# First layer's query and key weights multiplied into one matrix on chip; V buffers zeroed by transfers

## The reference, cut to what matters

```python
h = film(rmsnorm(x, norm1_w), cond, film1_w, film1_b)      # x * (1 + scale) + shift, per batch entry
Q = h @ q_w + q_b
K = h @ k_w + k_b
V = h @ v_w + v_b
scores = jnp.einsum('bnd,bmd->bnm', Q, K) * D ** (-0.5)
attn = jax.nn.softmax(scores, axis=-1)
out = jnp.einsum('bnm,bmd->bnd', attn, V)
x = x_in + (out @ proj_w + proj_b)
```

## Time and profile before

| | us |
|---|---|
| median of 3 runs | 182.25 |
| lowest and highest | 182.13, 182.42 |
| the profiled execution | 182.43 |
| its span in the trace | 180.7 |

### The profile page before, as it was taken

One profiled execution on the slowest core, in us unless ns is written; L12 is line 12 of the kernel. 1 busy time (PEld: TensorE's weight loads), 2 busy tenths in 40 slices (PEclk: granted clock), 3 DMA queues, 4 the chain that ended last, 5 costly groups with the idle time before them and its releaser, 6 DMA issues.

```text
span 180.7 us, 5691 instructions
## 1 busy us (share of the span) xinstructions
PE 172.1 (95%) x2250; PEld 133.9 (74%) x2250; DVE 116.0 (64%) x349; ACT 107.7 (60%) x274; POOL 107.5 (59%) x176
## 2 busy tenths in 40 slices
PE   6988999999999999989999999999899999999994
PEld 6965888587485798767678876888788765668594
DVE  0694569978106069867756878768688556696333
ACT  2338858871993651667576766767877596623500
POOL 5499979899910905995005333359979877690000
PEclk9999999999999999999999999999999999999999
DMA  4999999702247200300110001100000000001103
GB/s 111 341 425 429 424 421 426 337 13 39 51 175 308 102 0 4 120 7 3 62 39 32 2 5 64 64 2 5 5 7 7 5 0 5 0 0 58 62 0 116
DMA packets 5334, 19.31 MB, mean 107 GB/s; under 512 B 572, under 2 KB 1292, under 8 KB 3980
## 3 DMA queue, kind: packets, MB, share of 16 engines
q1 hardware_dynamic: 4988, 18.27, 26.2%
q10 hardware_dynamic: 320, 0.68, 1.2%
HBM read 7.24 MB, written 1.09 MB: 46 GB/s over the span
## 4 chain that ended last, share of the span: by engine, by line
PE 47%; POOL 26%; issue 17%; DVE 6%; DMA 3%; ACT 0%; POOLq 0%; ACTq 0%
PE ps L328 8%; PE ps L337 7%; PE ps L315 6%; PE ps L307 6%; PE ps L265 4%; POOL gtmp L1222 4%; POOL xb L1224 4%; POOL xc L1217 3%; POOL xn L1252 3%; POOL rstd L1143 3%; PE ps L239 3%; POOL xs L1231 3%; DMA xs<-x 3%; POOL gated L1228 3%; PE ps L270 2%
## 5 line engine op out<-in xcount | busy, mean ns | idle before, releaser
L1028 DVE TENSOR_REDUCE nm<-ps 128x4 f32<-128x512 f32 x64 | 42.1, 683 | 17.1 <-PE ps L380 16.6
L765 ACT ACTIVATE shared<-ps 128x512 f32<-128x512 f32 x64 | 34.5, 596 | 18.8 <-PE ps L380 18.8
L380 PEld LDWEIGHTS ps<-k_pad,q_pad 32*128 32x128 f32 x512 | 29.7, 186 | 9.7 <-issue 5.9
L380 PE MATMUL ps<-k_pad,q_pad 32*128 32x128 f32 x512 | 35.0, 282 | 1.7 <-DVE nm L1028 1.3
L380 PE MATMUL ps<-q_pad,k_pad 32*128 32x128 f32 x512 | 35.0, 283 | 0.0
L380 PEld LDWEIGHTS ps<-q_pad,k_pad 32*128 32x128 f32 x512 | 29.3, 186 | 0.4 <-issue 0.2
L1143 POOL TENSOR_TENSOR rstd<-var_eps,half 128x4 f32<-128x4 f32 x16 | 16.4, 1025 | 20.9 <-DVE var_eps L886 15.2
L1228 POOL TENSOR_TENSOR gated<-attn,gate 128x128 f32<-128x128 f32 x16 | 7.3, 459 | 27.2 <-ACT attn L784 27.2
L446 PE MATMUL ps<-shared,vx 128*32 128x128 f32 x512 | 17.3, 275 | 0.3
L813 ACT ACTIVATE hid<-ps,W 128x512 f32<-128x512 f32 x16 | 10.9, 688 | 9.7 <-PE ps L328 9.7
L446 PEld LDWEIGHTS ps<-shared,vx 128*32 128x32 f32 x512 | 13.1, 109 | 3.0 <-issue 1.5
(11 more groups left out here) (135 smaller groups left out, 330.6 us busy)
## 6 DMA issues: line engine op xcount, KB each, us to landing
q_pad<-hid SPq DMA_DIRECT2D x1, 4096.0 KB, 21.9
k_pad<-hid SPq DMA_DIRECT2D x1, 4096.0 KB, 30.9
gate<-gates SPq DMA_DIRECT2D x1, 2048.0 KB, 6.6
xs<-x SPq DMA_DIRECT2D x4, 256.0 KB, 6.6
gate<-mask SPq DMA_DIRECT2D x1, 1024.0 KB, 11.8
q_pad<-apT SPq DMA_DIRECT2D x4, 256.0 KB, 2.4
k_pad<-apT SPq DMA_DIRECT2D x4, 256.0 KB, 2.4
W<-weights SPq DMA_DIRECT2D x1, 768.0 KB, 9.9
```

Source lines behind the costliest of these rows:

```text
L380: return mm(bank(to)[:, t], held[some, t, b], moved[some, t, b], start=True, stop=True, skip_group_check=True)
L765: a(pT[b % 2][:, r], bank(of), ACT.Exp, scale=HD ** -0.5).then_inc(s["c_exp"], 1)
L1028: v.tensor_reduce(nm[b % 2][:, 4 * r:4 * r + 4], bank(of), AX.X, ALU.max, negate=True).then_inc(s["c_max"], 1)
```

## The change

- **Weights.** The packed weights hold the transposes of Q's and K's weights. At the start PE multiplies them: `key_mat` is the product of the two matrices, `query_key` is K's weights times Q's bias, `key_row` is Q's weights times K's bias, and `query_bias` is the product of the two biases. The scores are then (h M + query_key) h plus a term for each row of the scores, and no K is computed: the scores' second operand is `hT` itself.
- **Key bias.** It adds a constant to each row of the scores. It comes out of V's product as its 129th column. The fourth entry of V lies in another bank (2), since four times 129 columns don't fit one.
- **Row maximum.** PSUM holds the scores without the row term; VectorE takes the maximum, then computes from it the true maximum (`amax`) and back from that the offset for the exponential (`emax`), two small instructions (`a_true`), after a wait for V's copy. ScalarE now evicts the query (it was VectorE) and V in two instructions, V of group 0 after the affine of group 1.
- **Start.** The folding products stand before the first transposes on PE, and ScalarE copies their result before its first affine. Group 1's normalisation is split between GpSimd and ScalarE. GpSimd makes both bias columns before its first root.
- **V buffers.** The two memsets of `vx` on GpSimd go. SyncE fills both buffers by two transfers of 1024 KB, issued behind the fills of the pads and ahead of the wait for all of them. The zeros lie in the upper half of `gate` instead of `hid[1]`, so ScalarE's wait for the fills goes. GpSimd waits for all four fills and writes the ones after its fourth layer-0 bias addition.

```diff
@@ SyncE
-            zeros = hid[1][:].rearrange("p f b n -> p (f b n)")
+            zeros = gate[:, B // 2:B].rearrange("n b g c -> n (b g c)")
             sp.wait_ge(s["zero_ok"], 1)
             for to in (q_pad, k_pad):
                 sp.dma_start(to[:].rearrange("p t b n -> p t (b n)"), zeros.unsqueeze(1).broadcast_to((128, 4, B * N)))\
                     .then_inc(s["pad_zero"], 16)
 
-            sp.wait_ge(s["pad_zero"], 32)
+            for to in vx:
+                sp.dma_start(to[:].rearrange("n b z -> n (b z)"), zeros).then_inc(s["pad_zero"], 16)
+
+            sp.wait_ge(s["pad_zero"], 64)
             sp.wait_ge(s["aug_ok"], 3)
@@ TensorE
-            def a_qk(g, n):
-
-                if n == 0:
-                    pe.wait_ge(s["a_h"], g + 1)
-                    pe.wait_ge(s["a_hd"], 1)
-                mm(ps[:, 1 + n, :], w("qk"[n]), hT[g % 2][:], start=True, stop=True).then_inc(s[("a_Q", "a_K")[n]], 1)
+            def a_query(g):
+
+                pe.wait_ge(s["a_h"], g + 1)
+                pe.wait_ge(s["a_hd"], 1)
+                pe.wait_ge(s["fold_ok"], 1)
+                if g:
+                    pe.wait_ge(s["a_qT"], g)
+                mm(ps[:, 1, :], key_mat, hT[g % 2][:], start=True, stop=True).then_inc(s["a_Q"], 1)
 
             def a_value(g):
                 pe.wait_ge(s["wvp_ok"], 1)
+                if g:
+                    pe.wait_ge(s["a_v"], g)
                 for j in range(G):
-                    ins = mm(bank(3)[:, j], hT[g % 2][:, j], wvp[:], start=True, stop=True, skip_group_check=True)
+                    to = ps[:, 3, 129 * j:129 * j + 129] if j < 3 else ps[:, 2, 0:129]
+                    ins = mm(to, hT[g % 2][:, j], wvp, start=True, stop=True, skip_group_check=True)
                 ins.then_inc(s["a_V"], 1)
 
             def a_scores(g):
                 u = g % 2
                 pe.wait_ge(s["a_qT"], g + 1)
-                pe.wait_ge(s["a_kT"], g + 1)
                 for j in range(G):
-                    ins = mm(bank(4 + 3 * u)[:, j], qT[u][:, j], kT[u][:, j], start=True, stop=True, skip_group_check=True)
+                    ins = mm(bank(4 + 3 * u)[:, j], qT[u][:, j], hT[u][:, j], start=True, stop=True, skip_group_check=True)
                 ins.then_inc(s["a_S"], 1)
                 pe.wait_ge(s["a_v"], g + 1)
...
             warm(6)
+            pe.wait_ge(s["w_attn0"], 16)
+            pe.wait_ge(s["qcol_ok"], 1)
+            at = 2 * N
+            for lhs, rhs, size in ((w("qt"), col("cols0", COL["k_b"]), 1), (w("qt"), w("kt"), C),
+                                   (w("kt"), col("cols0", COL["q_b"]), 1), (qcol[:], col("cols0", COL["k_b"]), 1)):
+                ins = mm(ps[:, 6, at:at + size], lhs, rhs, start=True, stop=True, skip_group_check=True)
+                at += size
+            ins.then_inc(s["fold_mm"], 1)
             a_first_norm()
...
-            a_qk(0, 0)
-            a_qk(0, 1)
+            a_query(0)
+            pe.wait_ge(s["a_xa"], 1)
+            a_norm(1)
             a_value(0)
-            a_norm(1)
             a_scores(0)
             for g in range(3):
-                a_qk(g + 1, 0)
-                a_qk(g + 1, 1)
+                a_query(g + 1)
                 a_value(g + 1)
@@ ScalarE
+            def a_q(g):
+                act.wait_ge(s["a_Q"], g + 1)
+                a(qT[g % 2], bank(1), ACT.Identity, bias=query_key).then_inc(s["a_qT"], 1)
+
+            def a_v(g):
                 act.wait_ge(s["a_V"], g + 1)
-                a(v0[g % 2][:], bank(3), ACT.Copy).then_inc(s["a_v"], 1)
+                a(v0[g % 2][:, 0:3], ps[:, 3, 0:387].rearrange("n (b c) -> n b c", b=3), ACT.Copy)
+                a(v0[g % 2][:, 3], ps[:, 2, 0:129], ACT.Copy).then_inc(s["a_v"], 1)
...
+            act.wait_ge(s["fold_mm"], 1)
+            a(folded[:, C:2 * C + 3], ps[:, 6, 2 * N:3 * N + 3], ACT.Copy, scale=C ** -0.5).then_inc(s["fold_ok"], 1)
             act.wait_ge(s["film_ok"], 2)
             affine("a_", 0, 0, bank(0), range(2))
             act.wait_ge(s["wvp_mm"], 1)
-            a(wvp[:], ps[:, 6, 0:C], ACT.Copy).then_inc(s["wvp_ok"], 1)
-            a_kv(0)
+            a(wvp[:, 0:C], ps[:, 5, 0:C], ACT.Copy).then_inc(s["wvp_ok"], 1)
+            act.wait_ge(s["a_pow"], 2)
+            for j in range(2, G):
+                ins = a(xn[1][:, j], xs[:, G + j], ACT.Copy, scale=rstd[:, 0, G + j:G + j + 1])
+            ins.then_inc(s["a_xa"], 1)
+            a_q(0)
             affine("a_", 1, 0, bank(0))
+            a_v(0)
             a_exp(0)
@@ VectorE
             def a_max(g):
                 u = g % 2
                 dve.wait_ge(s["a_S"], g + 1)
                 v.tensor_reduce(amax[:, u, :], bank(4 + 3 * u), AX.X, ALU.max, negate=True).then_inc(s["a_max"], 1)
+                dve.wait_ge(s["a_max"], g + 1)
+                dve.wait_ge(s["a_v"], g + 1)
+                row_term = v0[u][:, :, C]
+                v.scalar_tensor_tensor(out=amax[:, u, :], in0=amax[:, u, :], scalar=query_bias, in1=row_term,
+                                       op0=ALU.subtract, op1=ALU.subtract).then_inc(s["a_true"], 1)
+                dve.wait_ge(s["a_true"], 2 * g + 1)
+                v.scalar_tensor_tensor(out=emax[:, u, :], in0=amax[:, u, :], scalar=query_bias, in1=row_term,
+                                       op0=ALU.add, op1=ALU.add).then_inc(s["a_true"], 1)
@@ GpSimd
-            norm(0, 0, "a_", range(2))
-
             pool.wait_ge(s["ident_ok"], 2)
             pool.wait_ge(s["w_film"], 16)
+            p.tensor_scalar(qcol[:], ident[:], 0.0, col("cols0", COL["q_b"]), ALU.mult, ALU.add).then_inc(s["qcol_ok"], 1)
             p.tensor_scalar(bcol[:], ident[:], 0.0, col("cols0", COL["v_b"]), ALU.mult, ALU.add).then_inc(s["bcol_ok"], 1)
-            norm(0, 1, "a_")
+            norm(0, 0, "a_", range(2))
+            norm(0, 1, "a_", range(2))
...
-            for u in range(2):
-                p.memset(vx[u][:].rearrange("n b z -> n (b z)"), 0.0).then_inc(s["c_vinit"], 1)
-            pool.wait_ge(s["c_vinit"], 2)
...
             next_bias(3)
+            pool.wait_ge(s["pad_zero"], 64)
+            for t in vx:
...
```

More of the change, by code:

```diff
@@ L77, in build @@
         shared = sb("shared", [128, 8, G, N])
-        qT, kT, v0, p0 = ([shared[:, 2 * n + u] for u in range(2)] for n in range(4))
+        qT, p0 = ([shared[:, n + u] for u in range(2)] for n in (0, 6))
+        flat = shared.rearrange("p a g n -> p (a g n)")
+        v0 = [flat[:, 1024 + 520 * u:1024 + 520 * u + 516].rearrange("p (g c) -> p g c", g=G) for u in range(2)]
+        folded = flat[:, 2064:2064 + 2 * C + 3]
+        wvp, key_row, key_mat, query_key, query_bias = (folded[:, a:b] for a, b in (
+            (0, C + 1), (C, C + 1), (C + 1, 2 * C + 1), (2 * C + 1, 2 * C + 2), (2 * C + 2, 2 * C + 3)))
         pT0 = [sb(f"apT{u}", [N, G, N]) for u in range(2)]
@@ L82, in build @@
         arden = sb("arden", [N, 2, G])
-        wvp = sb("wvp", [C, C])
+        qcol = sb("qcol", [C, N])
+        emax = sb("emax", [N, 2, G])
         bias_a = sb("bias_a", [N, C])
@@ L173, in _ @@
                 sp.dma_start(xs[:, G * g:G * g + G], x[:, G * g:G * g + G]).then_inc(s[f"x_in{g}"], 16)
-            for n, (a, b) in enumerate((("q", "x_end"), ("ada", "q1"), ("mlp1", "m_end"), ("q1", None))):
+            for n, (a, b) in enumerate((("qt", "x_end"), ("ada", "q1"), ("mlp1", "m_end"), ("q1", None))):
                 a, b = W_AT[a], W_AT[b] if b else W_ALL
@@ L290, in a_weighted @@
                 for j in range(G):
-                    ins = mm(bank(6)[:, j], pT0[g % 2][:, j], v0[g % 2][:, j], start=True, stop=True, skip_group_check=True)
+                    ins = mm(bank(6)[:, j], pT0[g % 2][:, j], v0[g % 2][:, j, 0:C], start=True, stop=True, skip_group_check=True)
                 ins.then_inc(s["a_PV"], 1)
@@ L666, in _ @@
             a = nc.scalar.activation
-            act.dma_start(W[:, 0:W_AT["q"]], weights[:, 0:W_AT["q"]]).then_inc(s["w_film"], 16)
+            act.dma_start(W[:, 0:W_AT["qt"]], weights[:, 0:W_AT["qt"]]).then_inc(s["w_film"], 16)
             act.dma_start(R[:, :], rows.partition_broadcast(128)).then_inc(s["rows_in"], 16)
@@ L931, in _ @@
             dve.wait_ge(s["rows_in"], 16)
-            v.tensor_tensor(bias_a[:], ps[:, 5, 0:C], row("proj_b"), ALU.add).then_inc(s["bias_ok"], 1)
+            v.tensor_tensor(bias_a[:], ps[:, 7, 0:C], row("proj_b"), ALU.add).then_inc(s["bias_ok"], 1)
             dve.wait_ge(s["x_in2"], 16)
             statistics(0, 2)
-            def a_q(g):
-                dve.wait_ge(s["a_Q"], g + 1)
-                v.tensor_scalar(qT[g % 2][:], bank(1), col("cols0", COL["q_b"]), C ** -0.5, ALU.add, ALU.mult)\
-                    .then_inc(s["a_qT"], 1)
             def a_max(g):
@@ L1177, in _ @@
             bias_add(3, bias_a[:], s["a_xb"])
-            for u in range(2):
-                p.memset(vx[u][:].rearrange("n b z -> n (b z)"), 0.0).then_inc(s["c_vinit"], 1)
-            pool.wait_ge(s["c_vinit"], 2)
```

(11 more changed lines are left out.)

29 lines of the change are left out of this document (11 added, 18 removed).

## The result

The changed kernel takes 187.49 us (median of 4 runs, 186.94 to 188.88) beside 182.33 us for the kernel before on the same chip: a ratio of 1.028, 95% interval 1.023 to 1.033. It is slower, as forecast, but by 5.2 us and not by 2.6, and it lies above the range. The profiled execution took 186.94 us, 185.2 of them its span; before, the span was 180.7.

The account below looks back on a forecast made before the run. PE was taken to bound the kernel, with SyncE's queue ending 1.2 us before it. Span 180.7 + 2.6 of wait = 183.3, plus 1.7 around it = 185.0, less 0.18 to the median: 184.8 us, range 183.7 to 186.0.

Parts of the forecast that it names:

- The wait: PE at layer 1's first scores waits for the K spread: 64.2 us instead of 61.59, 2.6 us later.
- part 1: Layer 0 attention, one matrix in place of Q and K: stage end between 1.1 us earlier and no gain.
- The steps in between: SyncE's queue from fills to spreads: mask rows out 42.3, gates out 47.7, back 56.3, broadcast landed 62.9, K spread 64.2.
- What this does to the rest: Everything behind layer 1's first scores: PE-bound, so the 2.6 us wait stays whole, with nothing given back.
- The rival that PE slows down after standing still: Behind PE's wait, some 5.7 us at half pace cost 2.8 us: 187.6 us; chance 0.05.
- the end of the stage: Weighted sum of group 3 in layer 0's attention, then at 36.97 us: some 1.1 us earlier without collisions.
- the collisions: Layer 0: small VectorE instructions stall behind GpSimd's bias adds, up to 1.3 us lost in each of groups 0 and 1.
- Part 2 and 3: Start folding: first transposes end about half a microsecond later. V zeroed by transfers: memset removal worth nothing, queue 4.9 us later.
- Rival 1: SyncE's queue has more room, no wait appears: 181.2 us (chance 0.08) or, with VectorE collisions, 182.2 (0.07).
- point of decision: At layer 1's first scores, PE waits only if the gates' broadcast slips by over 2.3 us.
- Rival 4: In SyncE's queue, each fill pays its own start: 6.8 us more, 191.6 us; chance 0.02.

Follow-up runs that it names:

- e3: Changed kernel with the first spreads of Q and K issued ahead of the gates' broadcast, both fills kept: 182.41 us, ratio 1.000.
- e2: Kernel before with only the V-buffer part of the change (two SyncE fills, none of the new layer 0 arithmetic): 188.06 us, ratio 1.027.
- e1: Changed kernel without its V-buffer part, GpSimd's memsets zeroing both V buffers at their old place: 182.31 us, ratio 0.998.
- e12: e1 without the two small VectorE instructions and without the key bias, so e10's layer 0 with memsets and the old queue: 180.49 us, ratio 0.989.
- e5: Changed kernel with one V buffer filled by SyncE and the other zeroed by a GpSimd memset: 182.28 us, ratio 1.000.
- e9: e3 without the two small VectorE instructions behind each maximum: 180.06 us, ratio 0.984.
- e6: Changed kernel with both fills issued behind the gates' way out, GpSimd's wait for them left where it was: 194.77 us, ratio 1.059.
- e7: e6 without the two small VectorE instructions behind each maximum: 193.76 us, ratio 1.064.
- e11: e6 with GpSimd's wait for the fills behind its first four layer-1 normalisations and the first spreads ahead of the gates' broadcast: 182.17 us, ratio 0.998.
- e4: Changed kernel with 20 throw-away PE passes ahead of PE's wait for the spreads: 185.94 us, ratio 1.015.
- e8: e7 with the key bias left out, V 128 columns wide and two folding products: 194.28 us, ratio 1.065.
- e10: e9 with the key bias left out, V 128 columns wide and two folding products: 179.77 us, ratio 0.984.

## Why the prediction was right, and where it failed

**The wait: right, partly by luck.** First scores were forecast at 64.2 and came at 64.25, by a DMA into k_pad, with the mechanism of the text: e3 removes it by moving the broadcast, and e2 shows it without part 1. The steps in between were less exact. The wait for the fills ended at 42.78 (forecast 42.3: the fills cost 5.4 us, the upper bound). The mask rows took 1.5 us and not 3.4, which I had copied from the earlier trace rows; sent out at 37.3, they took 3.2 us in e1 and 1.5 in e12, so this time varies from run to run. The gates went out at 46.18 (47.7) and came back at 54.40 (56.3). The broadcast was priced at the 6.6 us of the earlier trace rows and took 8.4 with the two spreads in flight. So 62.8 for its landing against 62.9: an error of -1.9 and one of +1.8. The spreads then landed behind the broadcast in turn, as I had it: 62.8, 63.5, 64.1. The two errors before them cancelled by luck.

**The step that failed: "What this does to the rest".** It gave back nothing and took nothing more: the term for what PE's stop costs behind the first scores stood at nothing. It measured 1.84 us in the changed kernel and 2.7 in e2, all of it clock. The rival that PE slows down after standing still had a chance of 0.05 and was what happened, beside the forecast wait. Its evidence was at hand, with 20 passes at 0.23 us and 12 at 0.13, but I discounted it because the granted clock read 1.00 in the earlier trace rows: stretches of 28 and 70 us, which don't include the start, and in which PE never stood still for 2 us, can't show what such a stop does. Nor could the clock at the start have shown it: e5's reads 1.00 from 7.5 to 10.2 us, where its 12 passes take 2.91 us. The two costs belonged into one case, for whoever forecasts a wait of 2.6 us forecasts its after-effect as well. By the sum with it, 185.0 + 1.84 = 186.8 for the profiled execution, which was 186.94; with its 2.8 us for the clock my rival said 187.6, and the median was 187.49, which is luck in part, since 2.8 was 1 us too much for the profiled execution. The range should have reached there. The median is 0.55 us above the profiled execution; what makes the changed kernel's runs differ by 1.9 us wasn't settled. A late start, as in e5, is a candidate: the kernel before has times of 182.0 to 182.6 and of 183.7 to 184.2 us. No trace of the changed kernel's two longer executions was kept. The longer wait in e2's profile (3.12 against 2.48 us) came with a larger clock cost (2.7 against 1.84), which would widen any scatter in the wait.

**Part 1: right on its weaker side.** The forecast put the end of the stage between -1.1 us and nothing, and within 0.1 us of 36.97 with the collisions; the weighted sum of group 3 starts at 36.48 in e1 and 36.40 in e3, and the time can't tell the 0.5 us. ScalarE's query step starts at 11.98 in e1 (forecast 12.2), and the collisions stand where they were forecast, though the second costs 0.4 us and not up to 1.3. V's two instructions take 0.51 and 0.30 us with some overlap, within 0.60 to 0.98. What I mis-sized is the price of the small pair: I had 0.4 us a round and some 1.0 for the collisions, of which VectorE's other work would hide a part, while without the pair the stage ends at 34.64 (e9), 2.3 us before 36.97, and most of what the pair took in the first two rounds is still there at the end. In the changed kernel's own profile PE stands 1.06 us for the weights, until 8.78, and the granted clock is 0.58 at 12.3 to 15.2; the weighted sum of group 3 is at 37.20, 0.23 later than before. It is hidden by the later wait.

**Part 2 and 3.** The folding cost less than forecast: in e1 the first transposes start at 9.22 against 8.98 before, 0.24 us later and not half a microsecond (9.69 in the changed kernel's own profile, behind its wait for the weights). That the memsets are worth nothing held with this layer 0 (e1 against e3) and not with a faster one: 0.75 us in e12. GpSimd's new wait was met on arrival in the changed kernel, as forecast; e6 and e7 show what hung on it.

**The rivals and the page.** Rival 1 (room in the queue) would have been right with one fill (e5) or with the other order (e3): its point of decision, a broadcast later by 2.3 us, fits both: the broadcast is issued 0.4 us later than before in e5 (51.81 against 51.38), which doesn't wait (in a profile with a late layer 0), and 3.0 later in the changed kernel (54.40), which does. Rival 4 is out: two fills moved the queue by 5.4 us, not by 6.8 or more. The Trainium skill's 2.0 us of fixed time for each DMA ("DMA: Bandwidth & Descriptors", section "Anatomy of one DMA — SWDGE (gpsimd) path") would have made the fills 8.9 us by my estimate from it; they took 5.4 in a queue that was already full, so here the measurement decides against adding it.

## What to carry to other kernels

A DMA queue whose transfers wait for each other is a chain of its own, and the chain of waits doesn't show it until it is too late by more than its room; here the room was between 0.4 and 3.0 us at the issue of the gates' broadcast, the lower figure from e5's late execution: one 1024 KB fill passed under it, two didn't. Where a change adds to such a queue, look for the small urgent transfer behind the large patient one and swap them (e3), and put the wait for a transfer behind all that its engine owes to others (e11). A wait of PE of 2.5 us cost the wait and then 1.84 us of clock; and before a correction is added to every round, ask whether the next operation cancels it: without the row term's two instructions the same kernel is 1.6% faster than before, with them it is level.

## What the runs showed of the hardware

- **PE's clock after a wait.** After 2.48 us idle the scores ran 1.2 us at full clock and the drop to 0.50 came behind them; after 3.12 us idle (e2) it was there at once. In e7, after 9.62 us idle, it read 0.50 from 58.7 to 64 us. The costs were 1.84 and 2.7 us in the first two, and the mean clock stayed at 1.00 where passes filled the idle time (e4). The Trainium skill says in "TensorE: Matmul & The Clock Gate", section "What's actually happening", that the throttled state is the default and activity releases it; the traces agree, 0.50 behind the idle stretch and 1.00 by 70 us, with PE busy throughout. At the start of the kernel the 12 warm-up passes took 1.58 us in most traces and 2.91 in those of e4, e5 and e8; in e4 and e5 PE's first query product came some 2.2 us later than in e3.
- **Small instructions behind GpSimd.** 1.31 us for a 0.23 us VectorE instruction, until GpSimd's 1.27 us addition ended. The Trainium skill describes it in "SBUF — State Buffer", section "🔬 SBUF: two separate sides": the port pair the two engines share is held by one of them for its whole instruction. The trace agrees, and shows that 4 values in a partition suffice to be held up.
- **A small transfer behind a large one lands behind it.** Two 256 KB spreads issued 3.1 and 3.8 us after a 2048 KB broadcast took 6.0 and 5.9 us and landed 0.7 and 1.3 us after it; issued 2.2 and 1.5 us before it landed (e4) they took 2.9, and 2.4 when they came later than that or ahead of it. The broadcast took 8.4 us there (8.5 in e2) against 6.6 to 7.2 in the kernel before, e1, e4, e5 and e12, but it also took 7.4, 8.8 and 8.6 in e3, e9 and e10, where the spreads went ahead of it. What lengthens it wasn't tested.
- **A fill behind small transfers is slow.** 1024 KB took 12 us (median of two) in e7 and e11 behind the mask rows and the gates. The gates' 16 KB took 8.2 us in the changed kernel, and 10.8 and 10.4 in e7 and e11 with the fills behind them. The DMA engines weren't idle: in e7 their busy share was 1.03 at 203 GB/s from 45 to 49 us, and 1.05 at 435 GB/s from 58.7 to 61. By what they were held wasn't tested.
